# Finer order of the stack transfers in two long attentions of a twelve-stage decoder kernel

## What is computed

```python
# stage 7, memory attention: 8 heads of 16, queries are x itself, masked
p = softmax(q @ k_ctx.T * 16**-0.5 + mask); out = p @ v_ctx
# stage 10, cross-self attention: 16 heads of 8, keys and values are those of the context and x's own
q, k, v = split(x @ w_qkv.T)
k = concatenate([k_ctx, k]); v = concatenate([v_ctx, v])      # 1601 + 256 = 1857 keys
p = softmax(q @ k.T * 8**-0.5); out = (p @ v) @ w_proj.T + b_proj
```

## Time and profile before

| | us |
|---|---|
| median of 3 runs | 4905.21 |
| lowest and highest | 4900.76, 4919.58 |
| the profiled execution | 4897.87 |
| its span, first to last instruction | 4896.1 |
| PE busy | 4044.6 (83%) |
| DVE busy | 3492.3 (71%) |
| ACT busy | 2513.1 (51%) |
| POOL busy | 1396.9 (29%) |
| mean granted TensorE clock | 0.899 of full |

### The profile page before, as it was taken

One profiled execution on the slowest core, in us unless ns is written; L12 is line 12 of the kernel. 1 busy time (PEld: TensorE's weight loads), 2 busy tenths in 40 slices (PEclk: granted clock), 3 DMA queues, 4 the chain that ended last, 5 costly groups with the idle time before them and its releaser, 6 DMA issues. The chain is left out here.

```text
span 4896.1 us, 77611 instructions
## 1 busy us (share of the span) xinstructions
PE 4044.6 (83%) x29323; PEld 2220.6 (45%) x29323; DVE 3492.3 (71%) x5389; ACT 2513.1 (51%) x3544; POOL 1396.9 (29%) x1033
## 2 busy tenths in 40 slices
PE   5659796999999999999968986848995768888883
PEld 3645334666656666666643333423443432222231
DVE  5469444899897777878764455757774658888868
ACT  2133242666666666666641233534663446777772
POOL 0000300677776666666657012000000100000000
PEclk5579897999999999999978997978996788999996
DMA  0024001111110000000013016325540433223300
GB/s 19 1 104 161 40 0 45 47 48 41 44 45 1 14 1 14 14 1 1 1 60 135 0 38 137 49 46 83 83 63 4 100 73 57 50 45 57 49 2 9
DMA packets 144610, 218.52 MB, mean 45 GB/s; under 512 B 20442, under 2 KB 109036, under 8 KB 143556
## 3 DMA queue, kind: packets, MB, share of 16 engines
q1 hardware_dynamic: 136548, 197.22, 17.4%
q0 software_dynamic: 6528, 16.42, 1.4%
q10 hardware_dynamic: 1184, 0.12, 0.0%
HBM read 154.00 MB, written 56.69 MB: 43 GB/s over the span
## 5 line engine op out<-in xcount | busy, mean ns | idle before, releaser
L3116 POOL TENSOR_TENSOR arena<-arena 128x512 f32<-128x512 f32 (+1 forms) x768 | 1149.5, 1498 | 528.2 <-ACT arena L3072 468.1
L2544 ACT ACTIVATE arena<-ps 128x1024 f32<-128x1024 f32 (+1 forms) x688 | 703.3, 1023 | 318.6 <-PE ps L2469 307.8
L3132 DVE TENSOR_TENSOR arena<-arena 128x1024 f32<-128x1024 f32 (+1 forms) x448 | 703.8, 1607 | 7.9 <-ACT arena L3099 5.9
L2562 DVE TENSOR_REDUCE arena<-ps 128x2 f32<-128x826 f32 (+1 forms) x576 | 564.8, 981 | 167.0 <-PE ps L2415 159.1
L3157 DVE TENSOR_TENSOR arena<-ps,arena 128x512 f32<-128x512 f32 (+1 forms) x768 | 527.8, 689 | 118.7 <-ACT arena L3066 87.5
L2415 PE MATMUL ps<-arena 48*128 48x413 bf16 (+3 forms) x1920 | 432.2, 331 | 132.4 <-DVE arena L2562 67.8
L3066 ACT ACTIVATE arena<-ps 128x1024 f32<-128x1024 f32 (+1 forms) x448 | 411.0, 960 | 214.6 <-PE ps L2993 214.6
L3072 ACT ACTIVATE arena<-arena 128x1024 f32<-128x1024 f32 (+1 forms) x448 | 429.6, 993 | 107.0 <-DVE arena L3132 104.2
L2993 PE MATMUL ps<-arena 64*128 64x256 f32 (+1 forms) x3328 | 425.2, 391 | 18.8 <-ACT arena L3094 12.4
L2488 PE MATMUL ps<-arena 128*9 128x256 f32 (+2 forms) x5504 | 430.9, 385 | 10.9 <-ACT arena L2532 8.0
L2974 PE MATMUL ps<-arena 128*128 128x256 f32 (+1 forms) x1664 | 419.6, 384 | 0.8 <-DVE arena L3140 0.8
(11 more groups left out here) (649 smaller groups left out, 5847.6 us busy)
## 6 DMA issues: line engine op xcount, KB each, us to landing
wide_keys<-arena SPq DMA_DIRECT2D x27, 800.5 KB, 3.5
arena<-wide_keys SPq DMA_DIRECT2D x27, 800.5 KB, 4.3
arena<-in_ctx_feat SPq DMA_DIRECT2D x12, 1601.0 KB, 10.6
arena<-ctx_parts SPq DMA_DIRECT2D x96, 200.1 KB
arena<-ctx_parts SPq DMA_DIRECT2D x192, 100.1 KB
arena<-in_ctx SPq DMA_DIRECT2D x16, 768.0 KB
arena<-diff_att_stack SPq DMA_DIRECT2D x60, 192.0 KB
ctx_parts<-arena SPq DMA_DIRECT2D x24, 400.2 KB, 3.8
```

What stands on the lines that cost most here:

```text
L2544: act.activation(self.prob[0:rows, u % 3, :], self.ps[0:rows, 2 * (u % 2):2 * (u % 2) + 2, :].rearrange("p n c -> p (n c)"), ACT.Exp).then ...
L2562: ins = dve.tensor_reduce(dst[:, :, j // 2], self.ps[:, 4:6, 0:hi - lo], AX.X, ALU.max)
L3116: pool.tensor_tensor(acc[0:rows, u % 2, :], before, sc[0:rows, u % 2, t, :], ALU.add).then_inc(added, 1)
L3132: dve.tensor_tensor(e, e, mb[0:rows, u % 2, None, :].to_broadcast([rows, n, 2 * S]), ALU.subtract).then_inc(sub_done, 1)
```

## The change

`sp_unit` becomes `sp_stacks` (one half `e` of a unit's stack) and `sp_values`. In stage 10 the half for partitions 0 to 63 follows the max rows of a unit's first group and the half for partitions 64 to 127 those of its second; the values follow the second half. With one lane (stage 7) a half is the whole. At the start of both stages SP stores the first chunk only, waits for it, fetches unit 0's slices and then stores the rest; the wait for the rest stands ahead of unit 4. In stage 10 the second half of unit 0's token slices is issued by POOL, counted by a semaphore of its own, and PE's wait for `own_copied` moves from ahead of the looks to ahead of the first scores.

```diff
--- before.py
+++ after.py
@@ -2295,6 +2295,7 @@
         self.lead = 12
         self.moves = lanes
         self.units = self.groups // lanes
+        self.half = 0
         c = -(-2 * nk // 9)
         self.both = [(i * c, (i + 1) * c) for i in range(3)]
         self.alone, self.left_over = (3 * c, 4 * c), (4 * c, nk)
@@ -2313,7 +2314,7 @@
         self.ones = st.sb("ones", [32, nk], BF16)
         names = ("ones_ready", "ones_loaded", "v_loaded", "v_ready", "stacks_loaded", "s_ready", "s_free", "split_ready", "turned_max",
                  "rows_ready", "max_loaded", "st_ready", "exp_done", "pv_done", "o_copied", "back_turned", "out_done",
-                 "bank_clear", "dve_own")
+                 "bank_clear", "dve_own", "half_loaded")
         self.sem = {n: st.sem(n) for n in names}
         self.ident_h = st.sb("ident_h", [P, P], BF16)
 
@@ -2340,7 +2341,7 @@
         return g * self.steps - self.lead * self.steps // self.looks + 2
 
 
-    def run_pool(self, pool, spans):
+    def run_pool(self, pool, spans, first=None):
         s = self.sem
         pool.memset(self.ones[:, :], 1.0).then_inc(s["ones_ready"], 1)
         pool.wait_ge(s["ones_ready"], 1)
@@ -2353,6 +2354,8 @@
             if self.lanes == 1:
                 pool.dma_start(self.qst[self.rows - PARTS:self.rows, r, :, :],
                                self.ones[0:PARTS, None, 0:S].to_broadcast([PARTS, 4, S])).then_inc(s["ones_loaded"], 16)
+        if first:
+            first()
         pool.memset(self.vh[:, :, :, :, self.hd:self.hd + 1], 1.0).then_inc(s["ones_ready"], 1)
         pool.wait_ge(s["ones_ready"], 2)
         for b in range(B):
@@ -2365,20 +2368,20 @@
             ins.then_inc(s["v_ready"], 1)
 
 
-    def sp_unit(self, sp, w, stacks, values):
+    def sp_stacks(self, sp, w, e, stacks):
         s = self.sem
-        if w:
-            sp.wait_ge(s["stacks_loaded"], w * self.loads * 16)
-        if w >= 4:
-            sp.wait_ge(s["st_ready"], (w - 3) * self.lanes * self.steps)
-        stacks(w)
-        if w % 2 == 0:
-            b = w // 2
-            if b:
-                sp.wait_ge(s["v_loaded"], b * self.v_loads * 16)
-            if b >= 2:
-                sp.wait_ge(s["v_ready"], b - 1)
-            values(b)
+        if e == 0:
+            sp.wait_ge(s["stacks_loaded"], (w * self.loads - self.half) * 16)
+            if w >= 4:
+                sp.wait_ge(s["st_ready"], (w - 3) * self.lanes * self.steps)
+        stacks(w, e)
+
+    def sp_values(self, sp, b, values):
+        s = self.sem
+        sp.wait_ge(s["v_loaded"], b * self.v_loads * 16)
+        if b >= 2:
+            sp.wait_ge(s["v_ready"], b - 1)
+        values(b)
 
     def sp_rows(self, sp, g):
         s = self.sem
@@ -2390,13 +2393,16 @@
                          self.max_rows[e * per:(e + 1) * per, :]).then_inc(s["max_loaded"], 16)
 
     def run_sp(self, sp, stacks, values):
-
-        self.sp_unit(sp, 1, stacks, values)
+        self.sp_stacks(sp, 1, 0, stacks)
         for g in range(self.groups):
             self.sp_rows(sp, g)
+            if g == 0 and self.lanes == 2:
+                self.sp_stacks(sp, 1, 1, stacks)
             w = self.unit(g) + 2
-            if g % self.lanes == 0 and w < self.units:
-                self.sp_unit(sp, w, stacks, values)
+            if w < self.units:
+                self.sp_stacks(sp, w, g % self.lanes, stacks)
+                if g % self.lanes == self.lanes - 1 and w % 2 == 0:
+                    self.sp_values(sp, w // 2, values)
 
 
     def pe_look(self, pe, n):
@@ -2404,7 +2410,9 @@
         g, i = n // self.looks, n % self.looks
         ring = self.unit(g) % 4
         if i == 0 and g % self.lanes == 0:
-            pe.wait_ge(s["stacks_loaded"], (self.unit(g) + 1) * self.loads * 16)
+            pe.wait_ge(s["stacks_loaded"], ((self.unit(g) + 1) * self.loads - self.half) * 16)
+            if g == 0 and self.half:
+                pe.wait_ge(s["half_loaded"], self.half * 16)
         if n >= 2:
             pe.wait_ge(s["s_free"], n - 1)
         pair, qt, j = i // 12, i // 6 % 2, i % 6
@@ -2490,7 +2498,7 @@
                             start=(t == 0), stop=(t == self.steps - 1))
         ins.then_inc(s["pv_done"], 1)
 
-    def run_pe(self, pe):
+    def run_pe(self, pe, banks_free=None):
         total = self.groups * self.steps
         turns = {self.turn_step(g): g for g in range(1, self.groups)}
         backs = {(g + 1) * self.steps + 2: g for g in range(self.groups - 1)}
@@ -2501,6 +2509,8 @@
         self.pe_turn_max(pe, 0)
         for n in range(self.looks, self.looks_by(0)):
             self.pe_look(pe, n)
+        if banks_free:
+            pe.wait_ge(banks_free, 1)
         for u in range(total):
             self.pe_scores(pe, u)
             for n in range(self.looks_by(2 * u), self.looks_by(2 * u + 1)):
@@ -2673,8 +2683,10 @@
                 load_stack(sp, s["stacks_loaded"], att.qst[:, w % 4, :, :], HD2, 0,
                            lambda k: q_parts[k, h0:h0 + 4 * HD2, b * S:(b + 1) * S])
 
-            def stacks(w):
+            def stacks(w, e):
                 context(w)
+                if w == 4:
+                    sp.wait_ge(stored, chunks * PARTS * 16)
                 queries(w)
 
             def values(b):
@@ -2682,14 +2694,17 @@
                 sp.dma_start(att.v[:, b % 2, 0:full, :], src[0:full * P, :].rearrange("(t p) d -> p t d", p=P)
                              ).then_inc(s["v_loaded"], 16)
                 sp.dma_start(att.v[0:rest, b % 2, full, :], src[full * P:SC, :]).then_inc(s["v_loaded"], 16)
-            context(0)
-            for i in range(chunks):
+            def store(i):
                 for n, ready in enumerate((high_ready, mid_ready, low_ready)):
                     sp.wait_ge(ready, i + 1)
                     sp.dma_start(q_parts[n, :, i * BANK:(i + 1) * BANK], part_q[:, i, n, :]).then_inc(stored, 16)
-            sp.wait_ge(stored, chunks * PARTS * 16)
+            context(0)
+            store(0)
+            sp.wait_ge(stored, PARTS * 16)
             queries(0)
             values(0)
+            for i in range(1, chunks):
+                store(i)
             env.fetch_weights(sp, 8)
             att.run_sp(sp, stacks, values)
 
@@ -3555,40 +3570,44 @@
                 sa, H3, HD3, len(TERMS) * HD3, 2, tiles, KX,
                 out_of=lambda b, h0: branch[:, b * BT:(b + 1) * BT, h0 * HD3:(h0 + 4) * HD3])
             s = att.sem
-            att.loads, att.v_loads = 6 * len(TERMS), 3
+            att.loads, att.v_loads, att.half = 6 * len(TERMS), 3, 2 * len(TERMS)
             chunks = T // BANK
             rest_qk = sa.sb("rest_qk", [P, 4, BANK])
             part_qk = sa.sb("part_qk", [P, 2 * chunks, PARTS, BANK], BF16)
             projected, high_ready, rest_ready, mid_ready, low_ready, stored, own_ready, own_copied = (
                 sa.sem(n) for n in ("projected", "high_ready", "rest_ready", "mid_ready", "low_ready",
                                     "stored", "own_ready", "own_copied"))
+            first_stored = sa.sem("first_stored")
 
             def place_qk(i):
 
                 return (i % 2) * 4 + i // 2
+
+            def sides(w):
+                return [(slice(64 * e, 64 * (e + 1)), lambda t, e=e: t.rearrange(
+                    "(w s e d) t -> w e d s t", w=2, e=2, d=HD3)[w % 2, e]) for e in range(2)]
+
+            def tokens(eng, loaded, w, e):
+                b, r = w // 2, w % 4
+                rows, side = sides(w)[e]
+                load_lane(eng, loaded, att.qst[rows, r, :, :], HD3, 0,
+                          lambda k: side(q_parts[k, :, b * S:(b + 1) * S]))
+                load_lane(eng, loaded, att.kst[rows, r, :, SC:KX], HD3, 1,
+                          lambda k: side(own_parts[k, :, b * S:(b + 1) * S]))
             block = sa.block()
 
             @block.sync
             def _(sp):
-                sides = lambda w: [(slice(64 * e, 64 * (e + 1)), lambda t, e=e: t.rearrange(
-                    "(w s e d) t -> w e d s t", w=2, e=2, d=HD3)[w % 2, e]) for e in range(2)]
-
-                def context(w):
-                    for rows, side in sides(w):
-                        load_lane(sp, s["stacks_loaded"], att.kst[rows, w % 4, :, 0:SC], HD3, 1,
-                                  lambda k: side(env.ctx_parts[k, w // 2]))
-
-                def tokens(w):
-                    b, r = w // 2, w % 4
-                    for rows, side in sides(w):
-                        load_lane(sp, s["stacks_loaded"], att.qst[rows, r, :, :], HD3, 0,
-                                  lambda k: side(q_parts[k, :, b * S:(b + 1) * S]))
-                        load_lane(sp, s["stacks_loaded"], att.kst[rows, r, :, SC:KX], HD3, 1,
-                                  lambda k: side(own_parts[k, :, b * S:(b + 1) * S]))
-
-                def stacks(w):
-                    context(w)
-                    tokens(w)
+                def context(w, e):
```

(32 more changed lines are left out.)

## The result

The changed kernel takes 4886.86 us (median of 7 runs, 4878.16 to 4891.95) where the kernel before, timed beside it on the same chip, takes 4913.85 (7 runs, 4900.76 to 4922.89). The ratio is 0.9944, 95% interval 0.9930 to 0.9958: some 27 us, or 0.56%, faster. That lies inside the range I gave, just beyond the 0.5% that I called the limit of "same", and where rival A stood (4885.0), not where the forecast stood (4895.6). The profiled execution took 4880.26 us.

What follows compares the result with a forecast made beforehand. Waits at both attention starts and late max rows in steady cross-self attention were to go: 8.6 + 3.2 + 8.4 - 10.6 = 9.6 us of gain, from 4905.21 to 4895.6. Forecast band 4888 to 4902 (0.50), range 4881 to 4912.

Steps and rivals of the forecast that it cites:

- rival A: Steady cross-self attention: values land clear of VectorE's split, giving 20.2 us of gain, 4885.0 us; chance 0.27.
- The late max rows: Steady cross-self attention: TensorE's waits on max rows and the clock falls behind them go away, gaining 8.4 us.
- The collisions: Steady cross-self attention: POOL's value copies meet VectorE's split of the maxima; five meetings and about three clock falls cost 10.6 us.
- one of my own signs of being wrong: Steady cross-self attention: POOL's value copies falling past 17.7 us after odd groups' max rows would show the forecast wrong.
- rival B: Steady cross-self attention: all seven copies meet the split, the clock falling each time, 3.8 us each: 4911 us; chance 0.11.
- The starts: Starts of both attentions: waiting for fewer stores before fetching token slices gains 8.6 us in cross-self and 3.2 in memory.
- the landing of the first six stores: Cross-self start: the wait for the first query and key chunks ends at 4012.5, between bounds of 4011.1 and 4013.2.
- POOL's half comes last: Cross-self start: POOL issues its 12 token slices in 6.6 us, landing 2.1 later, after SP's half; first look at 4021.2.
- Memory: Memory attention's start: waiting for 3 stores instead of 12 gains 3.2 us, between 2.0 and 4.3.
- Costed at nothing: Pieces moved behind the starts, such as later stores, unit 1's late half and POOL's memset, were taken as hidden: no cost.
- C: Cross-self start gains nothing: POOL's half lands 11.5 us after issue or first stores drain last; 4905.0 us, chance 0.06.
- D: Steady waits aren't cured, as even groups' max rows now follow the values: 8.4 us missing, 4904 us; chance 0.06.

Runs made afterwards that it cites:

- halves only: Changed kernel with both starts put back as before, stacks still sent by halves with values behind the second: 4891.49 us against 4911.28, ratio 0.9950.
- values early: Changed kernel with cross-self values sent between context and token slices of the second half: 4914.29 us, ratio 1.0005; with POOL's copy also waiting for the split, 4880.39.
- Stores between: Changed kernel with the first chunk's stores moved between the two halves of unit 0's context slices, in both attentions: 4884.36 us, ratio 0.9950.
- starts only: Changed kernel with both new starts, but whole stacks sent behind the max rows of a unit's first group, as before: 4904.95 us, ratio 0.9986.
- ones late: Changed kernel with POOL's eight cross-self transfers of ones sent behind its token slices, awaited ahead of the first scores: 4883.99 us against 4905.73, ratio 0.9959.

## Why the prediction was right and wrong

**The late max rows: mechanism right, size right for the profile read, too small for the kernel.** I put 8.4 us on them. The two profiled executions differ by 8.51 in the interval sum, the waits are gone and the clock doesn't fall. But halves only gained 19.8 us, and the other execution of before has an interval sum of 693.38, 25 us above the changed kernel's. The step that failed is the one where I took the loss from one execution and the start from the median: the medians of this study put that kernel at 4905.73 to 4913.85, and the execution read at 4897.87 was fortunate in this term above all. The two intervals of 24.96 and 24.82 were a sample of a wait that varies from batch to batch.

**The collisions: the step behind the wrong forecast.** I subtracted 11.0 us, half of the long burst, from a phase of 26.9, and had the copies at 15.9 us, on the split; I charged 10.6. None met it, and all seven are past 17.7, one of my own signs of being wrong. The six steady ones start 19.4 us after their rows on average, 3.5 later than I had them. The step that failed is the subtraction, and it fails in two places. Of the 11.0 us only 9.7 came off ahead of the values: SP begins to issue them 7.96 us after the rows on average, and in the kernel before it did so after 17.63. And from there to the copy it is 11.4 us, where it was 9.2. In the batch whose windows stand above, the nearest of the six, 1.5 us of rows, 9.0 of half a stack and 7.5 of values make 18.0, where my subtraction had 11.0 for the half stack and 4.9 (26.9 - 22.0) for rows and values together. I treated transfers that overlap as if they stood in a row. The phase that I subtracted from was a fortunate one as well: in the second execution of before the six copies start 28.9 us after an even group's rows on average, not 26.9, and 11.0 off that would have been 17.9, clear of the split.

The hold itself is as described: values early has six meetings and loses 29.5 us by them. There too my price was off: 4.9 us per meeting, not 1.0 with a fall in every second one, and not 3.8 at the most. So my rival B, priced right, was 20.2 - 7 x 4.9 = -14 us, and the changed kernel avoids it by 0.2 us in its nearest batch (0.3 in the second execution, whose nearest copy is at 17.96). Stores between, with the same steady order, did not avoid it in one batch. That the meetings are absent is the order's doing on the whole, but in the nearest batches it is luck.

**The starts: 11.8 predicted, 7.0 in the pair of profiles, 6.3 by starts only.** The step that failed is the landing of the first six stores: 21.9 us after the first context slice by my sum (4012.5 - 3990.64), 25.7 measured (4012.47 - 3986.79), and 23.4 to 25.7 over six executions with this start. I read SP's 11.16 us for three stores as full engines and added 1.4 us for them (4012.5 - 4011.1). The long issue is the ones' doing (3.5 us for all six without them in ones late, the contexts unchanged), and to the landing the ones add some 3.4 us. The clock readings of 4012.5 and of 4021 for the first look are met only because this execution began the stage 3.85 us earlier: counted from the first context slice the first look is at 34.72, where I had 30.6 and would have called 34.4 wrong. The rest of that term holds: POOL's half comes last, and lands within 2.3 us, where I took 2.1. Memory: 2.57 for 3.2. The pair of profiles understates the gain, as the execution of before was fortunate here too: three executions with the old start (the two of before and halves only) have their first look at 39.18, 41.98 and 42.29, six with the new one at 34.0 on average (32.71 to 34.72), so 7.2 for my 8.6; with the memory attention's 2.5 that makes 9.6 for 11.8.

**Costed at nothing and so measured:** POOL's memset, the wait for the own values, the stores behind the first looks, unit 1's late half. TensorE waits for no stack at look 24 or 48, and the first interval is 26.09 as it was 26.11. In the changed kernel's second execution it is 28.28, and the cause of that is open.

**The rivals.** A came out, at 4885.0 for 4886.86, but by errors that cancel: the gain was 11.4 larger in the late rows (19.8 for 8.4) and 5.5 smaller in the starts (6.3 for 11.8), and the kernel before, timed beside the changed one, stood 8.6 higher than the median I started from. B, C and D did not: D's sign, a steady wait on the rows, is absent, and so is one half of C, POOL's slices landing 11.5 us after issue; its other half, first stores that drain late, came in part and costs 3.8 of C's 9.4 us (25.7 for 21.9). A forecast of 0.27 for A was low. The phase rested on one subtraction, and a copy at 17.7 or later was as near as one at 15.9; I wrote that and gave it half the weight.

## What to carry to other kernels

Read a wait that varies from batch to batch in more than one execution before pricing it: one profile showed 8 us of a loss that was 25 in the next, and the start and the phase of the copies varied by 2 to 3 us as well. When a transfer is moved out of a burst, time it alone; what was left over at the end of the burst is not its length. Where two engines can hold each other, a semaphore that keeps them apart costs nothing that shows (values early takes 33 us less with it than without), and makes the order of the transfers free to choose. An order that misses a meeting by 0.2 us isn't safe: in one execution of six it met.

## What the runs showed of the hardware

*One engine's transfers hold up the issue of another's.* POOL's eight transfers of ones are 43.5 KB each; in the list of DMA issues from 3985 to 4020 (KB each, median us from issue to landing) of the changed kernel:

```profile
arena<-arena POOLq DMA_DIRECT2D x8, 43.5 KB, 13.1
```

They move 348 KB, under a third of the contexts' 1.2 MB (12 of 100.1 KB), yet while they are under way SP needs 14.2 us (10.82 + 3.34) to issue six stores, against 3.5 without them. The delay shows as issue time on another engine's queue. No run tells whether it is the size of their packets, their number or their route that does it.

*A held operation is held again.* POOL's copy is three instructions back to back; VectorE's subtraction waited for the first (1.31 us) and the cast behind it for a later one (0.55). Holds of 1.3 us on average on a chain in which TensorE already waited 1.1 us cost 4.9 in the end, with the time at 1.2 GHz that follows. TensorE's clock stayed at 2.4 GHz through all waits of up to 1.1 us in the changed kernel's steady part. In that of the kernel before it fell after waits of 1.55 and 1.63 us and, in the second execution, after five of 1.91 to 3.66; in values early it fell after five of 2.26 to 2.76 and stayed after one of 1.74. So no single length of a wait divides the two.
